# Where SyncE stores the x product in a graph kernel's loop: behind two groups of row copies or behind all four

## The chip, the cores and the metric

The kernel runs on one core of one Trainium2 chip. The metric is the device time of one execution in microseconds (us), and lower is better.

## The reference

Two graph layers, each followed by a residual and a layer norm over 256 features, for 12,500 nodes and 200,000 edges that are sorted by destination. The loop that the change touches belongs to the first layer:

```python
ZU = jnp.einsum('nd,kdr->knr', Z, U)            # 4 heads of 16 columns
zs = ZU[:, src, :]
zd = ZU[:, dst, :]
logits = (zs * zd).sum(-1) / scale
seg_max = jax.vmap(lambda l: jax.ops.segment_max(l, dst, num_segments=N))(logits)
exp_l = jnp.exp(logits - seg_max[:, dst])
seg_sum = jax.vmap(lambda e: jax.ops.segment_sum(e, dst, num_segments=N))(exp_l)
alpha = exp_l / (seg_sum[:, dst] + 1e-16)
weighted = alpha[..., None] * zs
agg = jax.vmap(lambda w_: jax.ops.segment_sum(w_, dst, num_segments=N))(weighted)
...
DZ = Z_half @ Dmat.T
residual = Z_half - DZ @ Dmat
grad_step = Z_half + ETA * (residual @ Dmat)
return jax.nn.relu(grad_step - ETA * LAM)
```

What `grad_step` does to Z itself, without the neighbours' part, is one product of x with a 256x256 matrix. It doesn't depend on the edges, and the kernel works it off inside the edge loop, two tiles of 128 nodes at a time. That is "the x product".

## The kernel before

The edges are cut into 1,563 tiles of 128. With the changes from one tile of nodes to the next the work has 1,660 steps, in 52 blocks of 32 steps, and a block has four groups of 8 steps (g = 0 to 3). One period of the loop on TensorE, VectorE and ScalarE is one block b:

- TensorE turns the block's logits around (L1384), which marks the start of a period here. VectorE runs a chain of short scans over them, with small steps of TensorE between (L1387 to L1398), until the exponents' arguments are ready (L1012, semaphore `x_ready`). Between the steps of the chain TensorE transposes the next block's one-hots (L1335).
- TensorE multiplies two tiles of x (L1378), and ScalarE copies the product out of PSUM (L1617, `xmz_copied`). VectorE scans the sums of the block before (L931), weighs the source rows and splits them in three bf16 parts (L1026, L1031, L1036).
- TensorE expands the next block's destination rows (L1347, 24 matmuls for each of four groups) and adds this block's rows up (L1364, eight quarters). The order written out is: expand 0 and 1, add up quarters 0 to 3, expand 2, quarters 4 and 5, expand 3, quarters 6 and 7. Two quarters belong to a group of 8 steps, and `sums_ps` counts quarters. Then the next period begins.

The source rows come in two moves. GpSimd gathers them from `z_table` in HBM with indirect DMAs, one for each edge tile (L576), in groups of 8, into a ring of 32 slots. SyncE (SP) copies them from the ring to the place in `zs` of each step (L437, 8 DMAs for a group). It can do so only when TensorE has added up what stood there two blocks before, so `copy_steps` waits for `sums_ps`, and when the gathered tiles have landed. After it has issued the copies of a group it waits until those of the group before have landed, and counts `copied` (L418). GpSimd waits for that count before it starts the next 8 gathers into the slots that came free (L573). So a group's gathers start when SP is done with a certain group of copies.

SP runs down one list. A `turn` is its share of a block. The turn of block b also loads the resets of block b (L453), stores the x product of period b - 1, for which it waits until ScalarE has copied it in that period (L470, L471), and loads the x tiles for the next product (L460).

Of the kernel before, what the change touches and what calls it, by code (L numbers as in the profile page):

```python
# [60 lines left out]
NG = B // G  # L61
# [36 lines left out]
def spread(ap, axis, n):  # L98

    shape = list(ap.shape)  # L100
    shape[axis] = n
    return ap.broadcast_to(shape)
# [25 lines left out]
def program(nc, x, xT, src_rows, dst_rows, u, dmat, head_w, weight, attn_l, attn_r, out):  # L128
    ctx = ExitStack()
    with ctx:  # L130
# [239 lines left out]
        def rows_of(table, t, n):  # L370

            return table[bass.ds(t * P, n * P), :].rearrange("(t p) c -> p t c", p=P)
# [17 lines left out]
        def _(sp):  # L390
# [24 lines left out]
            def landed(h, g, uses):  # L415

                sp.wait_ge(gathered[h][g], 16 * G * uses)
                sp.nop(nofuse=True).then_inc(copied, 1)  # L418

            def copy_steps(b, h, g, uses):  # L420

                start = type(b) is int and b < 2
                if not start:
                    sp.wait_ge(sums_ps, (B // Q) * (b - 2) + (B // Q // NG) * (g + 1))
                _, slots = nc.values_load_multi_w_load_instructions(
                    irow[0:1, bass.ds(b * B + g * G, G)], engines=[mybir.EngineType.SP], min_val=0, max_val=RING - 1,
                    skip_runtime_bounds_check_because="the vector engine has made them numbers of slots")
                if start and b == 0 and g == 0:
                    sp.wait_ge(tiles_in[0], 16 * G)
                else:  # L430
                    need = [sp.value_load(needs[0:1, bass.ds((b * NG + g) * 2 + i, 1)], min_val=16 * G, max_val=16 * G * EG) for i in range(2)]
                    for i in range(2):
                        sp.wait_ge(tiles_in[i], need[i])
                    sp.nop(nofuse=True)
                here = G if not (type(b) is int and b == NB - 1) else min(G, REAL - b * B - g * G)
                for j in range(here):
                    sp.dma_start(zs[:, h, g * G + j, 0:KR], ring[:, bass.ds(slots[j], 1), :].rearrange("p a c -> p (a c)")  # L437
                                 ).then_inc(gathered[h][g], 16)
                if g >= 1:
                    landed(h, g - 1, uses)  # L440
                elif not (start and b == 0):
                    landed(1 - h, NG - 1, uses - 1 if h == 0 else uses)
# [9 lines left out]
            def load_resets(b, h):  # L452
                sp.dma_start(resets[:, h, 0:P], spread(reset_rows[bass.ds(b * B, B), :].rearrange("j (a e) -> j a e", a=1), 1, K)  # L453
                             ).then_inc(resets_in[h], 16)
# [4 lines left out]
            def load_tiles(n, h):  # L459
                sp.dma_start(xe[:, h, :, :], xT[:, :, bass.ds(n * YT * P, YT * P)].rearrange("c p n -> p c n")).then_inc(xe_in[h], 16)  # L460

            def turn(b, h, uses, store, load):

                for g in range(2):
                    copy_steps(b, h, g, uses)
                sp.wait_ge(x_ready, b - 1)
                load_resets(b, h)
                if store:

                    sp.wait_ge(xmz_copied, b - 1)  # L470
                    sp.dma_start(rows_of(xmz_table, (b - 2) * YT, YT), xmz.rearrange("p (t d) -> p t d", t=YT)).then_inc(xmz_out, 16)  # L471
                if load:
                    load_tiles(b - 1, 1 - h)
                for g in range(2, NG):
                    copy_steps(b, h, g, uses)

            for g in range(2, NG):
                copy_steps(0, 0, g, 1)
# [4 lines left out]
            with nc.sync.Fori(1, NB // 2 - 2) as i:  # L483
                for h in range(2):
                    turn(2 * i + h, h, i + 1, True, True)
            for b in range(NB - 4, NB):
                turn(b, b % 2, b // 2 + 1, b - 2 < NY, b - 1 < NY)
# [1274 lines left out]
```

## Time and profile before

| | |
|---|---|
| median of 3 runs | 3708.65 us (3697.53 to 3719.24) |
| the profiled execution | 3677.74 us, of which span 3675.2 us |
| PE busy in the span | 1971.2 us (54%) |
| DVE busy | 1919.5 us (52%) |
| ACT busy | 1168.6 us (32%) |
| POOL busy | 1728.5 us (47%) |
| periods of the edge loop | 52 starts of a period, 193.3 to 3206.2 us |

No engine is busy for much over half of the span. Idle time of an engine says nothing by itself: what counts is which wait ends last in a period. The times of a timeline are microseconds from the start of the span, and the engine called SPq is SP's queue of DMA issues.

### The profile page before, as it was taken

The numbers are of one execution on the slowest core, as the hardware profiler recorded it, in microseconds if no ns is written. First come the engines' busy times: TensorE is split into PE (matmuls) and PEld (weight loads), VectorE is DVE, ScalarE is ACT, GpSimd is POOL, SyncE is SP. The second block draws the span as 40 slices with busy tenths as digits, with TensorE's granted clock in tenths as the row PEclk, the third lists the DMA queues.
The fourth block names the chain that finished last, engine by engine and source line by source line (L and its number), as shares of the span: only waits on it lengthen the run. The fifth ranks groups of instructions, "written<-read, shape, count | busy, mean of one in ns | idle before, by whom it ended". The sixth has DMA issues, their size and how long they took to land. (4 is left out here: it accounts for less than half of the span.)

```text
span 3675.2 us, 61713 instructions
## 1 busy us (share of the span) xinstructions
PE 1971.2 (54%) x15251; PEld 1490.8 (41%) x15252; DVE 1919.5 (52%) x5864; ACT 1168.6 (32%) x3040; POOL 1728.5 (47%) x1832
## 2 busy tenths in 40 slices
PE   9345545454545445454545455464545454567776
PEld 9233333343434334343424243343433333444666
DVE  4444646454545546454545455464545454666477
ACT  1112323222232323322232233233232322334477
POOL 1544454445444444554544544445544444252662
PEclk7555555555555555555555555555555555577798
DMA  6212222121212212121212112121212121285343
GB/s 205 52 32 46 47 44 46 42 46 42 48 41 47 46 41 48 42 49 40 47 39 48 42 44 48 41 50 41 48 40 45 41 49 39 58 274 179 112 140 107
DMA packets 406593, 232.96 MB, mean 63 GB/s; under 512 B 284096, under 2 KB 371434, under 8 KB 406506
## 3 DMA queue, kind: packets, MB, share of 16 engines
q1 hardware_dynamic: 346666, 154.11, 15.4%
q0 software_dynamic: 59840, 77.87, 9.8%
q8 instruction: 33, 0.54, 0.1%
q14 instruction: 54, 0.44, 0.0%
HBM read 134.80 MB, written 42.55 MB: 48 GB/s over the span
## 5 line engine op out<-in xcount | busy, mean ns | idle before, releaser
L576 POOL DMA_INDIRECT arena<-z_table,sslot x1563 | 1492.0, 955 | 1646.2 <-SPq L418 1114.0
L1347 PE MATMUL bank<-arena 128*128 x4992 | 613.8, 222 | 637.7 <-issue 585.8
L1347 PEld LDWEIGHTS bank<-arena 128*128 128x128 bf16 x4992 | 457.5, 105 | 789.5 <-issue 697.0
L1584 ACT ACTIVATE arena<-bank 128x272 f32<-128x272 f32 x416 | 269.8, 661 | 1574.8 <-remote 970.4
L902 DVE TENSOR_TENSOR xin<-arena,bank 128x512 f32<-128x512 f32 x208 | 143.1, 688 | 1044.3 <-remote 588.2
L1561 ACT ACTIVATE acc<-xTb 128x68 f32 x1600 | 384.6, 312 | 306.6 <-issue 296.0
L1364 PE MATMUL bank<-xto,arena 128*128 128x68 bf16 x3328 | 321.6, 246 | 147.5 <-issue 147.4
L1335 PE MATMUL bank<-ident_b,arena 128*128 128x128 bf16 x1664 | 214.8, 310 | 339.4 <-remote 205.3
L1364 PE MATMUL bank<-arena 128*128 128x68 bf16 x1664 | 296.9, 243 | 120.2 <-issue 90.5
L1364 PEld LDWEIGHTS bank<-xto,arena 128*128 128x128 bf16 x3328 | 281.5, 132 | 166.9 <-issue 166.9
L1335 PEld LDWEIGHTS bank<-ident_b,arena 128*128 128x128 bf16 x1664 | 160.4, 141 | 399.6 <-remote 200.2
L893 DVE TENSOR_SCALAR arena<-iota_b,didx 128x128 bf16<-128x128 bf16 x1664 | 297.9, 263 | 20.2 <-issue 13.4
L931 DVE TENSOR_TENSOR_SCAN xTb<-bank,arena 128x198 f32<-128x198 f32 x612 | 273.2, 522 | 16.2 <-ACT acc L1561 10.3
L1364 PEld LDWEIGHTS bank<-arena 128*128 128x128 bf16 x1664 | 214.1, 129 | 156.8 <-issue 117.9
L1571 ACT ACTIVATE arena<-bank 128x1024 bf16<-128x1024 bf16 x208 | 209.4, 1007 | 83.5 <-remote 52.0
L1378 PE MATMUL bank<-mz,dspace 128*128 128x256 f32 x392 | 183.4, 617 | 0.0
L1031 DVE TENSOR_TENSOR xto<-arena 128x544 f32<-128x544 f32 x208 | 149.3, 718 | 0.0
L905 DVE TENSOR_REDUCE agn<-xin 128x32 f32<-128x512 f32 x208 | 142.7, 686 | 7.2
L1036 DVE TENSOR_TENSOR xto<-xto 128x544 bf16<-128x544 f32 x208 | 145.3, 719 | 0.0
L1026 DVE TENSOR_TENSOR arena<-arena,bank 128x512 f32<-128x512 f32 x208 | 137.5, 681 | 1.8
L632 POOL DMA_INDIRECT xin<-xmz_table,src x98 | 95.4, 973 | 84.8 <-SPq L529 28.2
L1378 PEld LDWEIGHTS bank<-mz,dspace 128*128 128x128 f32 x392 | 109.4, 307 | 16.4
(264 smaller groups left out, 2543.6 us busy)
## 6 DMA issues: line engine op xcount, KB each, us to landing
arena<-arena SPq DMA_DIRECT2D x1660, 32.0 KB
arena<-z_table,sslot POOLq DMA_INDIRECT x1563
dspace<-in_xT SPq DMA_DIRECT2D x49, 256.0 KB
xmz_table<-agn SPq DMA_DIRECT2D x49, 256.0 KB
xmz_table<-arena SPq DMA_DIRECT2D x14, 896.0 KB
arena<-in_x SPq DMA_DIRECT2D x13, 896.0 KB, 11.4
out<-arena SPq DMA_DIRECT2D x12, 896.0 KB
xin<-in_xT SPq DMA_DIRECT2D x8, 896.0 KB
```

The lines of the kernel that those rows point to most:

```text
L576: pool.indirect_dma_start(ring[:, e % RING, :], None, z_table, bass.IndirectOffsetOnAxis(ap=sslot[:, e:e + 1], axis=0)).then_inc(tiles_in[ ...
L893: last = V.tensor_scalar(onehot[:, h, j, :], iota_b[:, :], didx[:, h, j:j + 1], None, ALU.is_equal)
L931: part_done = V.tensor_tensor_scan(to[:, c0:c1, :].rearrange("p c j -> p (c j)"), same_row[:, 0:(c1 - c0) * (B + 1)], sums[:, c0:c1, :].re ...
L1031: V.tensor_tensor(rest[:, js, :], zs[:, h, js, :], top(zs[:, h, js, :]), ALU.subtract).then_inc(rest_ready, 1)
L1036: V.tensor_tensor(low[:, js, :], rest[:, js, :], top(rest[:, js, :]), ALU.subtract).then_inc(parts_ready, 1)
L1335: last = T.transpose(tr_ps[g % 2][:, u * P:(u + 1) * P], onehot[:, h, g * G + u, :], ident_b[:, :])
L1347: last = T.matmul(zd_ps[g % 2][:, u * KR:(u + 1) * KR], onehotT[:, g * G + u, :], z3[:, bass.ds(tiles[u], 1), s, :].rearrange("p a c -> p ...
L1364: last = T.matmul(sum_ps[q % 2][:, (u % Q) * AW:(u % Q + 1) * AW], onehot[:, h, u, :], parts[s][:, u % Q, :], start=(s == 0), stop=(s == Z ...
L1378: last = T.matmul(zd_ps[1][:, t * D:(t + 1) * D], xe[:, 1 - h, c, t * P:(t + 1) * P], mz[:, c, :], start=(c == 0), stop=(c == DC - 1))
L1561: A.activation(acc[:, bass.ds(tiles[u % G], 1), :].rearrange("p a c -> p (a c)"), state[:, :, 1 + u], ACT.Copy).then_inc(state_stored, 1)
L1571: A.activation(onehotT[:, g * G:(g + 1) * G, :].rearrange("p j e -> p (j e)"), tr_ps[g % 2][:, :], ACT.Copy).then_inc(oneT_ready, 1)
L1584: A.activation(sums[:, :, 1 + q * Q:1 + (q + 1) * Q].rearrange("p c j -> p j c"), sum_ps[q % 2][:, 0:Q * AW].rearrange("p (j c) -> p j c", ...
```

## The change

In each turn SP issues the copies of all four groups first, and only then waits for the x product, stores it and loads the next x tiles. Nothing is added or left out, and no other engine's list changes.

```diff
                 sp.wait_ge(x_ready, b - 1)
                 load_resets(b, h)
+                for g in range(2, NG):
+                    copy_steps(b, h, g, uses)
                 if store:

                     sp.wait_ge(xmz_copied, b - 1)
                     sp.dma_start(rows_of(xmz_table, (b - 2) * YT, YT), xmz.rearrange("p (t d) -> p t d", t=YT)).then_inc(xmz_out, 16)
                 if load:
                     load_tiles(b - 1, 1 - h)
-                for g in range(2, NG):
-                    copy_steps(b, h, g, uses)
```

## Rows read from the trace of the kernel before

**Rows 1.** The page: the costliest group, busy us, mean ns, idle before.

```profile
L576 POOL DMA_INDIRECT arena<-z_table,sslot x1563 | 1492.0, 955 | 1646.2 <-SPq L418 1114.0
```

**Rows 2.** Waits of SP's queue, 200 to 3200 us: total us, times, longest.

```profile
SPq L471 <- ACT agn L1617: 309.0, 35, 26.9
...
SPq L434 <- DMA arena<-z_table,sslot: 4.4, 6, 1.1
```

**Rows 3.** Busy time by windows: the whole edge loop, and five of its periods.

```profile
193.30:3206.20 3012.90, 1518.39 (x12632) 1124.34 (x12632) 1534.25 (x4729) 879.19 (x2432) 1435.04 (x1507) 0.54 0.20 44
...
1613.00:1672.50 59.50, 30.45 (x249) 22.50 (x249) 30.28 (x94) 17.79 (x50) 30.33 (x32) 0.50 0.21 45
...
1916.00:1961.10 45.10, 28.88 (x248) 21.85 (x248) 30.41 (x94) 19.53 (x58) 17.25 (x18) 0.54 0.21 48
2156.40:2204.20 47.80, 29.11 (x249) 22.04 (x248) 29.92 (x94) 17.58 (x51) 23.27 (x24) 0.54 0.22 48
3036.70:3104.30 67.60, 29.87 (x249) 22.06 (x248) 30.17 (x94) 18.08 (x51) 30.46 (x32) 0.53 0.18 40
3171.10:3206.20 35.10, 26.98 (x240) 21.03 (x240) 29.91 (x94) 16.58 (x50) 2.50 (x3) 0.50 0.11 25
```

The columns are: window, its length, and the busy us with the instructions of PE, PEld, DVE, ACT and POOL, then the granted clock of PE, the DMA share and GB/s.

**Rows 4.** Busy time by windows inside the period from 1613.0 us.

```profile
1620.50:1628.00 7.50, 2.10 (x16) 1.83 (x17) 2.84 (x19) 1.92 (x5) 4.95 (x6) 0.50 0.27 55
...
1633.00:1641.00 8.00, 5.74 (x55) 4.45 (x54) 7.90 (x17) 0.60 (x1) 6.17 (x7) 0.50 0.35 90
...
1652.50:1669.00 16.50, 1.77 (x9) 0.89 (x9) 0.00 (x0) 0.65 (x1) 11.35 (x12) 0.50 0.19 36
```

**Rows 5.** Timeline of SP's DMA issues in that period, and one of 3069 us.

```profile
1611.33 5.07 SPq L437 DMA_DIRECT2D arena<-arena  x8
1619.93 8.91 SPq L437 DMA_DIRECT2D arena<-arena  x8
1629.04 0.63 SPq L453 DMA_DIRECT2D xTb<-reset_rows  x1
1634.78 0.41 SPq L471 DMA_DIRECT2D xmz_table<-agn  x1
1641.45 5.47 SPq L437 DMA_DIRECT2D arena<-arena  x8
1649.73 7.62 SPq L437 DMA_DIRECT2D arena<-arena  x8
1670.92 5.08 SPq L437 DMA_DIRECT2D arena<-arena  x8
...
3069.06 0.39 SPq L471 DMA_DIRECT2D xmz_table<-agn  x1
```

**Rows 6.** Timeline of GpSimd in that period: first and last gathers.

```profile
1617.23 0.95 POOL L576 DMA_INDIRECT arena<-z_table,sslot  x1 [9.25 <-SPq L418]
...
1629.59 0.95 POOL L576 DMA_INDIRECT arena<-z_table,sslot  x1 [2.61 <-SPq L418]
...
1647.76 0.94 POOL L576 DMA_INDIRECT arena<-z_table,sslot  x1 [6.51 <-SPq L418]
...
1666.52 0.94 POOL L576 DMA_INDIRECT arena<-z_table,sslot  x1 [0.30 <-issue]
```

**Rows 7.** Timeline of VectorE in that period.

```profile
1629.71 0.29 DVE L1012 TENSOR_TENSOR xin<-bank,xin 128x128 f32<-128x128 f32 x1
...
1644.12 0.22 DVE L1054 TENSOR_SCALAR fac<-bank,first_col 128x4 f32<-128x4 f32 x1
```

**Rows 8.** Timeline of TensorE in that period.

```profile
1612.98 0.47 PE L1384 MATMUL bank<-ident,agn 128*128 128x128 f32 x1
...
1646.11 3.16 PE L1347 MATMUL bank<-arena 128*128 x24
...
1661.58 0.21 PE L1347 MATMUL bank<-arena 128*128 x1 [1.88 <-issue]
```

**Rows 9.** Busy time by windows of the gathers (L576) alone.

```profile
3036.70:3056.70 20.00, 15.06 (x16) 0.50 0.21 43
```

## The prediction

> **What bounds the kernel now.** The page comes first. No engine is busy for more than 54% of the span, so the loop is held by waits, and the costliest group on the page is GpSimd's gathers: 955 ns each, and most of their idle time ends with SP's count of landed copies [rows 1]. The windows come next. The edge loop takes 3012.9 us, 51 periods of 59.1 us, with 29.5 gathers in each [rows 3]. The five single periods have nearly the same work on PE, DVE and ACT and very different lengths. With 3 gathers (and no x product) a period takes 35.1 us, with 18 it takes 45.1, with 24 it takes 47.8, with 32 it takes 59.5, and with 32 at other places 67.6 [rows 3]. So a period is some 35 to 38 us of chained work plus what the gathers take away, and it matters where they fall.
>
> The windows inside one period show how they take it. From 1652.5 to 1669.0 us, under 12 gathers, PE gets 9 matmuls done in 16.5 us and DVE nothing [rows 4]. One matmul of the expansion stands alone, 1.88 us behind the one before, for which the profile has no reason but "issue", where 24 of them took 3.16 us a few us earlier [rows 8]. SP is slowed as well: eight copies take 5.07 us in the open and 8.91 or 7.62 us under gathers, and from the end of one group at 1657.35 to the next at 1670.92 it needs 13.6 us, where it took 3.5 us from 1616.40 to 1619.93 [rows 5]. The start of the slow time lags the first gather: gathers start at 1647.76 and PE goes on until about 1651. Its end lags the last one: 1666.52, and PE moves again at about 1669 [rows 4, 6]. So I take each run of 8 gathers as 10 us, of which the first 3.5 are free and 2.5 behind it are not, some 8 to 9 us of slow time. A run that directly follows another gets no free start.
>
> What a slow time costs depends on what it meets. Count from the period's start at 1613.0 [rows 8]. Up to `x_ready` at 17 (1629.99) a chain of short steps runs, and there it costs its full length: in the window from 7.5 to 15 PE got 16 matmuls and DVE 19 instructions done [rows 4]. From 17 to 31 DVE works through long instructions (1629.71 to 1644.12, [rows 7]) and PE has only two expansions and some adding to do. Under the gathers from 16.6 on, DVE is busy for 7.90 of 8.0 us and PE does 55 matmuls [rows 4]: this run is nearly free. Then PE has four quarters, two expansions and four quarters to do, some 12 us in the open, and the 16 gathers from 34.8 to 54.5 stop it. Of four runs of 8 one is free, one costs 8 us in the chain, and two cost some 16 us in front of the period's end. 36 and 24 make 60, as measured.
>
> **The change part by part.** No instruction is added or removed. In each turn one wait, one store and one load (0.41 us for the issue of the store, and the load is alike) move behind two groups of copies, 16 copy issues and two headers.
>
> The wait itself: SP stood in it for 309.0 us, 35 times, 8.8 us each [rows 2]. In this period SP is done with the resets at 1629.67 and stores at 1634.78, so 5.1 us [rows 5]. After the change groups 2 and 3 don't wait for it. What they then wait for is `sums_ps` of two blocks before, long reached, and gathered tiles. Those waits are 4.4 us in the whole loop now [rows 2]; a group needs the gathers that started three or four groups of copies earlier, so I take 0 to 1 us a period and keep 2 as the upper bound. The group that is moved up starts at about 1632.5 in place of 1641.45.
>
> Who is waiting for SP's copies? GpSimd, and nobody else near: DVE and PE read a block's last copies at the end of the period, 15 us after SP has issued them (1657.35, next period at 1672.5), and after the change they come sooner still. So 5.1 us saved on SP save nothing directly. They move gathers. The store and the load are late by some 20 us at most; the next product is wanted a period later, so that is 0, and if the cover went it would be at most the delay of one x product, 5 us a period.
>
> Where the gathers go. From one group 0 to the next SP takes 59.6 us (1611.33 to 1670.92, [rows 5]), so without the wait some 54.5, so SP runs ahead until another wait holds it. That is the wait of group 0 for the sums of the first two quarters that PE makes in the present period. The expansion behind the first four quarters starts at 33.1 [rows 8], so these sums are there at about 32, 15 us behind `x_ready`. From that moment (called 0) I walk through one turn with the durations above. SP: header 2.2, copies 5.1, first gathers at 8.3. PE, undisturbed, ends its period some 12 us after those sums (the period of 45.1 us, whose gathers were out of its way, less 33), just as the slow time sets in at 12. Group 1 is issued by 20, with gathers at 21; group 2 by 32, gathers at 33; group 3 by 45, gathers at 45.5. So slow times lie at 12 to 20, 25 to 32, 36.5 to 44.5 and 49 to 57. The chain to `x_ready` needs 17 - 7.5 = 9.5 us in the open. It starts at 12 and gets 0, 5 and 4.5 us in the gaps, 9.5 together. It ends either at about 36.5 or, if that gap is missed, at 45. In the first case the slow time from 36.5 is free, but the one from 49 meets PE's expansions, and the sums come at about 60. In the second DVE's 14.5 us run from 45 to 59.5, the last slow time is mostly free, and PE's remaining 3 to 5 us behind 57 put the sums at 60 to 64. The new period is thus 60 to 64 us in place of 59.5, or up to 69 where PE misses its end before 12 and loses the first slow time as well. I take 61.5, 2 us more: the two runs of gathers that met PE's last part now meet the chain, which is no cheaper, and the free run stays about as free. Periods with 24 gathers should move by as much. 49 turns store an x product: 49 x 2 = 98 us.
>
> The bounds. Upper: the period from 3036.7 has 16 gathers in its first 20 us [rows 9] and stores x at 32.4 in place of 21.8 [rows 5]; with 67.6 us [rows 3] it is 8 us longer than the common one. If half of the turns look like that, 24 x 8 = 192 us more, and if all do, 390. Lower: two free runs in place of one, 8 us less in a third of the turns, 130 us less. The sum is made for the profiled execution: 3677.7 + 98 = 3776. The median of the runs lies 31 us above it, so 3807; I round to 3800.
>
> By the Trainium skill (SBUF — State Buffer, "SBUF: two separate sides") a DMA can't be slowed by a compute instruction nor the other way round, and only GpSimd and VectorE lock each other out of a shared pair of ports. What stands in [rows 4] disagrees: TensorE, which by that page waits for nobody, issues 9 matmuls in 16.5 us. By the page the place of the gathers wouldn't matter and the change would be worth nothing, which is the second rival's time.
>
> **The rivals.** *Faster: SP's wait was holding the gathers back, and they land better.* GpSimd idles for 6.5 us before its gathers at 1647.76 [rows 6] because SP has waited for x and then copied group 2, and most of that is in the time in which DVE has its long instructions. If groups 2 and 3 are gathered in that stretch, two of four runs are free. It decides if SP does not run ahead to the sums but stays about 10 us earlier than now. A second free run is worth up to 8 us in 32; with a third to a half of the turns that is 130 to 190 us: about 3550. Against it: gathers from 28 on then join those before them without a free start, and SP's cycle of 54.5 us won't stay in step with a period of under 60.
>
> *No change: the gathers cost the same wherever they fall.* The period with 24 gathers and that with 32 cost 1.99 and 1.86 us for each gather. If only the number counts, and it stays, the time does: 3709. Against it stand two periods with 32 gathers each and 8 us between them [rows 3].
>
> *Much slower: all four runs meet the chain and PE's end.* It takes that PE misses its end by a microsecond when SP's group 0 is released by PE itself: 67 to 69 us a period, 8 x 49 = 390 us, about 4100. For it: the two events fall together in my walk. Against it: PE also feels 3.5 us of free start, and such a lock would repeat only in turns with all 32 gathers.
>
> **How the numbers follow.** Forecast (0.5 to 5% slower) 0.42, much slower 0.12, no change 0.13, faster 0.33. 0.5%, or 19 us, is about what a measurement of this kernel can tell. The forecast's own range is 3730 to 3900. For 8 in 10 I leave out most of the much slower case and the far end of the faster one: 3590 to 3970. Faster 0.33, same 0.13, slower 0.54.
>
> **What would show it.** In the profile after: SP's wait at L471 shrinks, and a wait of group 0 for `sums_ps` (L425, on PE L1364) takes its place; that row right means that SP ran ahead. The gathers of a period start in four separate runs and none of 16. The store of x lies 30 us or more behind a period's start instead of 22. PE's stretch behind the first four quarters is free of gathers. If SP still waits at L471 and never at L425, SP did not run ahead and the walk is wrong. If the runs of gathers lie in the 15 us behind `x_ready`, the faster rival holds. If waits at L434 reach some us a period, the ring of 32 slots sets the pace and my 0 to 1 us was wrong.

## The result and the profile after

The changed kernel takes 3798.88 us in the median of 3 runs (3791.43 to 3809.05), against 3708.65 before: a ratio of 1.0246 (95% interval 1.0185 to 1.0308). It is slower, by 90 us. The forecast was 3800, in a range of 3590 to 3970.

The profiled execution took 3791.43 us, span 3789.5. The edge loop, in the windows view with the columns of [rows 3], and then five stretches of its common period, which starts at 1602.9 us:

```profile
178.10:3317.30 3139.20, 1492.44 (x12632) 1126.50 (x12632) 1530.42 (x4729) 875.69 (x2432) 1437.23 (x1507) 0.53 0.19 42
...
1602.90:1666.20 63.30, 29.11 (x250) 22.33 (x249) 30.05 (x94) 17.36 (x49) 30.58 (x33) 0.53 0.19 43
1604.00:1621.50 17.50, 0.00 (x0) 0.00 (x0) 0.00 (x0) 0.87 (x2) 12.17 (x13) 0.50 0.20 41
1621.50:1629.40 7.90, 3.55 (x21) 2.36 (x22) 5.55 (x28) 5.49 (x21) 0.00 (x0) 0.50 0.15 32
1629.40:1641.00 11.60, 8.35 (x38) 5.62 (x36) 6.33 (x33) 5.69 (x19) 7.55 (x8) 0.50 0.19 38
1643.30:1655.00 11.70, 4.67 (x48) 3.75 (x48) 10.92 (x22) 0.14 (x1) 7.55 (x8) 0.61 0.26 67
1655.00:1666.20 11.20, 10.61 (x121) 9.11 (x121) 4.82 (x8) 3.64 (x6) 2.48 (x3) 0.50 0.13 29
```

The loop is 126.3 us longer (3139.2 against 3012.9, [rows 3]), with the same instructions and nearly the same busy times (PE 1492 us against 1518, the others within 4). It also began 15 us earlier (178.1 against 193.3), which nothing in the change touches. The span grew by 114.3. The common period went from 59.5 to 63.3 us. In its first stretch TensorE and VectorE don't issue one instruction in 17.5 us, while GpSimd issues 13 gathers. In the last one PE goes at full rate: 121 matmuls in 11.2 us, where [rows 4] had 9 in 16.5.

SP's waits from 200 to 3320 us (total us, times, longest):

```profile
SPq L425 <- PE bank L1364: 262.5, 37, 10.8
SPq L425 <- remote: 139.0, 13, 12.6
SPq L473 <- ACT agn L1617: 91.0, 23, 17.8
...
SPq L434 <- DMA arena<-z_table,sslot: 2.6, 4, 1.4
```

The wait for the x product (309.0 us in [rows 2], now at L473) fell to 91.0. In its place SP waits 401.5 us at L425, which is the wait for the sums of the present period. All of it is in front of group 0. Gathered tiles are waited for no more than before (2.6 us against 4.4).

The timelines of SP, of the starts of GpSimd's runs of gathers, of VectorE's `x_ready` and last step (L1012, L1054), and of PE's period starts:

```profile
1602.21 4.54 SPq L437 DMA_DIRECT2D arena<-arena  x8
...
1623.50 5.11 SPq L437 DMA_DIRECT2D arena<-arena  x8
1632.20 10.23 SPq L437 DMA_DIRECT2D arena<-arena  x8
...
1643.14 0.42 SPq L473 DMA_DIRECT2D xmz_table<-agn  x1
...
1657.18 5.11 SPq L437 DMA_DIRECT2D arena<-arena  x8
```

```profile
1600.16 0.94 POOL L576 DMA_INDIRECT arena<-z_table,sslot  x1 [11.77 <-SPq L418]
...
1629.43 0.94 POOL L576 DMA_INDIRECT arena<-z_table,sslot  x1 [9.60 <-SPq L418]
...
1643.26 0.94 POOL L576 DMA_INDIRECT arena<-z_table,sslot  x1 [4.15 <-SPq L418]
...
1663.11 0.94 POOL L576 DMA_INDIRECT arena<-z_table,sslot  x1 [10.12 <-SPq L418]
```

```profile
1637.49 0.29 DVE L1012 TENSOR_TENSOR xin<-bank,xin 128x128 f32<-128x128 f32 x1
...
1653.36 0.21 DVE L1054 TENSOR_SCALAR fac<-bank,first_col 128x4 f32<-128x4 f32 x1
```

```profile
1602.89 0.48 PE L1384 MATMUL bank<-ident,agn 128*128 128x128 f32 x1
...
1666.19 0.47 PE L1384 MATMUL bank<-ident,agn 128*128 128x128 f32 x1
```

Group 0 of the next turn is now copied at 1657.18, 9 us ahead of the period's end at 1666.19. Its release starts 8 gathers 3 us ahead of that end (1663.11, and 1600.16 for the period shown). Group 1 follows at full pace at 1602.21, and the 8 gathers it releases join the first 8: one run of 16 gathers until 1619.8, across the start of the chain. With `x_ready` taken at the start of L1012, it comes 34.6 us behind the period's start, against 16.7 before ([rows 7, 8]). The run from 1643.26 falls under VectorE's long instructions, and from `x_ready` to the end it takes 28.7 us, against 42.8.

The common period is no exception. With a period's start taken at L1384 and its `x_ready` at L1012, in 47 periods of each trace (the fourth to the fiftieth):

| | start to `x_ready`, mean | rest, mean | periods with over 22 us to `x_ready` |
|---|---|---|---|
| before | 18.3 us | 41.1 us | 7 |
| after | 31.7 us | 30.6 us | 40 |

The first part lost 13.4 us a period and the second won 10.5. The long ones, of over 22 us, are those that a long run of gathers meets. In the changed kernel's trace a run of more than 8 gathers (with under 1 us between two of them) reaches into the part up to `x_ready` in 40 periods, and these are the same 40. Before, it does so in 10 periods, and all 7 long ones are among them.

### The profile page after: what moved, and what is told of

Read it like the earlier page. It is cut to its first block, busy times and chain, and to the rows that moved or that the text cites. A ratio compares the mean times of both kernels' runs of the same rounds, so it can differ in the third digit from the quotient of the medians.

```text
span 3789.5 us, 61713 instructions
## 1 busy us (share of the span) xinstructions
PE 1924.7 (51%) x15251; PEld 1474.1 (39%) x15252; DVE 1915.1 (51%) x5864; ACT 1164.2 (31%) x3040; POOL 1729.0 (46%) x1832
## 4 chain that ended last, share of the span: by engine, by line
another core or an unknown queue 17%; PE 16%; DVE 10%; issue 7%; ACT 3%; ACTq 1%; DMA 0%; POOL 0%; DVEq 0%; POOLq 0%; SPq 0%
PE bank L1347 5%; PE bank L1364 3%; DVE arena L893 2%; PE bank L1502 2%; DVE xTb L931 2%; PE bank L1472 1%; PE bank L1492 1%; PE bank L1504 1%; PE bank L1378 1%; ACT arena L1661 1%; PE bank L1476 1%; ACT acc L1561 1%; DVE xto L1031 1%; PE bank L1335 1%
## 5 line engine op out<-in xcount | busy, mean ns | idle before, releaser
L576 POOL DMA_INDIRECT arena<-z_table,sslot x1563 | 1494.4, 956 | 1749.0 <-SPq L418 1227.9
L1347 PE MATMUL bank<-arena 128*128 x4992 | 598.5, 226 | 247.8 <-issue 201.9
L1347 PEld LDWEIGHTS bank<-arena 128*128 128x128 bf16 x4992 | 464.8, 107 | 390.4 <-issue 292.6
L1387 PE MATMUL bank<-ident,xin 128*1 128x128 f32 x104 | 30.5, 395 | 747.1 <-DVE xin L970 692.9
L970 DVE TENSOR_TENSOR_SCAN xin<-xTb,bank 128x128 f32<-128x128 f32 x52 | 21.9, 420 | 740.0 <-remote 728.1
L1364 PE MATMUL bank<-xto,arena 128*128 128x68 bf16 x3328 | 312.7, 246 | 31.0 <-issue 30.9
L1364 PEld LDWEIGHTS bank<-arena 128*128 128x128 bf16 x1664 | 215.1, 129 | 183.6 <-issue 91.4
```

The source lines that it names most:

```text
L576: pool.indirect_dma_start(ring[:, e % RING, :], None, z_table, bass.IndirectOffsetOnAxis(ap=sslot[:, e:e + 1], axis=0)).then_inc(tiles_in[ ...
L1347: last = T.matmul(zd_ps[g % 2][:, u * KR:(u + 1) * KR], onehotT[:, g * G + u, :], z3[:, bass.ds(tiles[u], 1), s, :].rearrange("p a c -> p ...
L1364: last = T.matmul(sum_ps[q % 2][:, (u % Q) * AW:(u % Q + 1) * AW], onehot[:, h, u, :], parts[s][:, u % Q, :], start=(s == 0), stop=(s == Z ...
```

## The experiments

Ratios are to the kernel before on the same chip, with a 95% interval. The medians of before there were 3660 to 3674 us. The changed kernel itself wasn't run again beside them.

**Groups 2 and 3 held back again, store and load left late.**

```diff
-                sp.wait_ge(x_ready, b - 1)
+                if store:
+                    sp.wait_ge(xmz_copied, b - 1)
+                else:
+                    sp.wait_ge(x_ready, b - 1)
                 load_resets(b, h)
                 for g in range(2, NG):
                     copy_steps(b, h, g, uses)
```

> The changed kernel, with the resets' load between groups 1 and 2 waiting for the x product of the present period (xmz_copied) instead of for x_ready of the one before. So groups 2 and 3 are held as in the kernel before, but store and load of x stay behind group 3. If the change costs time because SP runs ahead and its gathers land in the chain, the ratio to before is 0.995 to 1.005 and L425 holds SP for under 50 us. If the late store and load cost the time, the ratio stays at 1.02 or more.

Measured 3655.97 us, ratio 0.9949 (0.9897 to 1.0001). The waits of SP's queue:

```profile
SPq L453 <- ACT agn L1620: 288.6, 30, 27.3
SPq L434 <- DMA arena<-z_table,sslot: 14.2, 18, 1.4
SPq L425 <- remote: 13.6, 2, 12.2
SPq L425 <- PE bank L1367: 1.5, 5, 0.6
```

The wait for the product is back (288.6 us), the wait for sums is nearly gone (15.1 us), and so is the loss. In the common period the store now goes out about 47 us behind the start, later than in the changed kernel (40 us), and it costs nothing. So the late store and load are not the cause.

**Groups 2 and 3 held only until the present `x_ready`.**

```diff
-                sp.wait_ge(x_ready, b - 1)
+                sp.wait_ge(x_ready, b)
                 load_resets(b, h)
```

> The changed kernel, with the resets' load between groups 1 and 2 waiting for x_ready of the present period, which is some 5 us ahead of the product's copy. Groups 2 and 3 so come some 8 us sooner than before and can't come sooner than that. If it counts where the gathers land, more of them lie in VectorE's long instructions: ratio 0.97 to 0.995. If only running ahead to the sums costs, 1.00. If each us by which the groups come sooner costs, 1.005 to 1.02.

Measured 3755.07 us, ratio 1.0182 (1.0097 to 1.0267). Here my expectation of a gain fell. The ratio lies in the range that I had given for a cost of each us by which the groups come sooner, but the periods show another course. Groups 2 and 3 are copied at 25 and 33 us in place of 29 and 37, and with them group 0 comes at 54 to 55 in place of 58. That is enough for its gathers to begin before the period's end in part of the periods: 17 of 47 have over 22 us to `x_ready`, against 7 before and 40 after. Most of the other periods with 32 gathers take about 60 us, no less than before. The starts of gather runs in one of the bad periods, from 1827.8 us:

```profile
1824.74 0.95 POOL L576 DMA_INDIRECT arena<-z_table,sslot  x1 [11.19 <-SPq L418]
...
1867.46 1.32 POOL L576 DMA_INDIRECT arena<-z_table,sslot  x1 [23.00 <-SPq L418]
```

One run of 16 gathers over the start, again, and the period took 69.6 us.

**Store and load between the third and the fourth group.**

```diff
                 load_resets(b, h)
+                copy_steps(b, h, 2, uses)
                 if store:
...
                     load_tiles(b - 1, 1 - h)
-                for g in range(2, NG):
-                    copy_steps(b, h, g, uses)
+                copy_steps(b, h, 3, uses)
```

> Half of the change: store and load stand between group 2 and group 3. Group 2 isn't held by x, group 3 is. If SP's running ahead is what costs, SP still stops at x each period, the runs of gathers differ little from before, and the time is 3690 to 3740 us. If the time goes up with each group that is put ahead of the store, about 3750.

Measured 3667.6 us, ratio 1.0002 (0.9965 to 1.0039). SP still stops at x (252.9 us, 29 times), and 7 of 47 periods have a long chain, as before. Its copies stand at the places of before, but each place has the group that comes one further down the list: groups 1 and 2 around the period's start (at -1.8 and 7.6 us in the median), then the store, then group 3 at 29.4 and group 0 of the next turn at 37.2, some 22 us ahead of the period's end. So a group 0 that goes out early costs nothing by itself, and the cost doesn't grow group by group: half of the change is free. SP's list in its common period, from 1534.7 to 1595.2 us:

```profile
1532.98 5.07 SPq L437 DMA_DIRECT2D arena<-arena  x8
1538.49 0.63 SPq L453 DMA_DIRECT2D xTb<-reset_rows  x1
1542.47 9.69 SPq L437 DMA_DIRECT2D arena<-arena  x8
...
1556.75 0.41 SPq L472 DMA_DIRECT2D xmz_table<-agn  x1
...
1564.47 5.12 SPq L437 DMA_DIRECT2D arena<-arena  x8
1572.45 6.93 SPq L437 DMA_DIRECT2D arena<-arena  x8
```

The load of the resets (L453) marks the first of these groups as group 1, and the store (L472) the second as group 2.

**The other direction: store and load between the first and the second group.**

> The other direction: store and load of x between group 0 and group 1, so three groups of copies stand behind the wait for x. SP can run ahead less than before. If every place that keeps a wait for x within reach of SP is alike, the ratio is 0.995 to 1.01. If the place sets where the runs of gathers fall and the kernel before had a good one, it is 1.01 to 1.06.

The load of the resets stays behind group 1. Measured 3933.83 us, ratio 1.0775 (1.0693 to 1.0856), beyond the 1.06 that I had as the upper end, and by another mechanism than the one I had named. Who waited for SP's copies (total us, times):

```profile
  DVE xin L902: 817.0, 86
```

Before it was 23.4 us in 5 times. SP waits 776.2 us for x and has three groups to copy behind it, so VectorE waits for the copies themselves. The part behind `x_ready` is 4.3 us longer than before (45.4 us in the mean), and the part up to it 1.3.

**Group 0 held until the period's end.** The changed kernel, with this wait in `copy_steps`, and as its control the kernel before with the same:

```diff
-                    sp.wait_ge(sums_ps, (B // Q) * (b - 2) + (B // Q // NG) * (g + 1))
+                    sp.wait_ge(sums_ps, (B // Q) * (b - 2) + (B // Q if g == 0 else (B // Q // NG) * (g + 1)))
```

> The changed kernel, with group 0 of a turn waiting for all eight quarters of the sums of the present period instead of two. Groups 1, 2 and 3 are as early as the order allows. If the change costs because group 0 is copied some 5 us ahead of the period's end, so that 16 gathers run without a gap over the start of the chain, this takes the cost away though groups 2 and 3 still go ahead of the x product: ratio to before 0.98 to 1.005. If it costs because groups 2 and 3 go ahead of the x product, the ratio stays at 1.015 or more, and if the longer wait costs by itself, it is over 1.025.

> The kernel before with the same wait of group 0, as a control. Its group 0 is mostly copied at the period's end anyway (57 to 60 us behind the start), so I expect 0.99 to 1.005. If the longer wait costs by itself, it is 1.01 or more.

Measured: the changed order with the hold 3703.44 us, ratio 1.0088 (1.0051 to 1.0124); the order of before with the hold 3710.46, ratio 1.0103 (1.0066 to 1.0140). The hold costs about 1% by itself, more than I expected of it. The 1.0088 alone lies in none of the ranges that I had named; it is the control that decides. With the hold the two orders are alike, and the changed one loses nothing. What the hold takes away is not group 0's lead alone: SP issues the groups in order, so groups 0 to 3 of the changed order all come later than without it, at 2.1, 10.8, 24.1 and 40.8 us in place of -8.7, -0.7, 20.5 and 28.7. The starts of gather runs in its common period, which starts at 1514.6 us:

```profile
1522.79 0.94 POOL L576 DMA_INDIRECT arena<-z_table,sslot  x1 [16.99 <-SPq L418]
1535.93 0.94 POOL L576 DMA_INDIRECT arena<-z_table,sslot  x1 [3.35 <-SPq L418]
1563.82 0.94 POOL L576 DMA_INDIRECT arena<-z_table,sslot  x1 [7.81 <-SPq L418]
```

The first gathers come 8 us behind the start and no longer 3 us ahead of it. `x_ready` comes 11.5 us behind the start in the mean, and no period has over 22. The 16 gathers in one run from 1535.93 then fall into the second part. Against the kernel before, the first part is 6.8 us shorter and the second 8.0 longer (49.1 us in the mean), which is what the hold loses.

**The hold with the store between the third and the fourth group.**

> Store between groups 2 and 3 with the same wait of group 0. If the ends of periods are kept free of gathers by this and one group more comes in VectorE's long instructions, 0.97 to 0.995; if it does the same as without the wait, 1.00.

Measured 3657.68 us, ratio 0.9948 (0.9913 to 0.9983). It is half a per cent faster than the kernel before, at the upper end of what was expected. Why the hold costs 1% in the two kernels above and nothing here, I can't show.

**Half of the gathers left out.** In both kernels GpSimd fetches only every second edge tile (with a memset of the ring to zero at the start, and all thresholds cut accordingly):

```diff
-                for e in range(q * G, min((q + 1) * G, ET)):
+                for e in range(q * G, min((q + 1) * G, ET), 2):
```

> The kernel before with every second gather left out (edge tiles 1, 3, 5 of each group of 8 and so on are never fetched, their ring slots keep zeros; all copies, waits and other work stay). If gathers take time from the other engines, a period falls from 59 to about 45 us and the time to 2950 to 3100 us. If the rows' slow times have another cause than gathers, it stays above 3500.

> The changed kernel with the same half of the gathers left out. If the change costs because of where the gathers land, the distance to the kernel before with half the gathers shrinks from some 90 to at most 45 us. If the order on SP and its waits for the sums cost by themselves, the distance stays 90 us or more.

Measured: 2673.4 us for the order of before, ratio 0.7289 (0.7261 to 0.7318), and 2619.18 us for the changed one, ratio 0.7142 (0.7043 to 0.7240). The edge loops of the two:

```profile
138.80:2192.10 2053.30, 1477.65 (x12633) 1130.99 (x12633) 1525.21 (x4729) 860.21 (x2432) 717.13 (x754) 0.53 0.23 52
```

```profile
138.90:2137.80 1998.90, 1474.30 (x12633) 1126.78 (x12633) 1525.66 (x4729) 852.07 (x2432) 728.61 (x754) 0.54 0.23 53
```

All other engines do the same work in 2053 us in place of 3013. For 781 gathers left out the time fell by 993 us (3666.87 - 2673.4), 1.27 us for each, about the distance at which GpSimd issues them in a run (16 in 20.0 us, [rows 9]). And the change has turned its sign: with half of the gathers it makes the kernel 54 us faster, though SP waits for the sums there too (L426, 216.2 us). I had only expected the loss to shrink. The wait for sums, then, isn't what costs. Nor is the early place of the copies: they go out at -9.1 and -1.1 us there, as in the changed kernel, and `x_ready` comes at 13.3 us in the mean, with no period over 22.

## Why the prediction was right

**SP runs ahead until the sums of the present period hold it: right.** The row that I had named is there, 401.5 us at L425, all of it in front of group 0. The store went out about 40 us behind a period's start, and TensorE's stretch behind the first four quarters is nearly free of gathers, as I had written. Tiles were not the limit (2.6 us), and the late store and load cost nothing, as the run with the product's hold shows.

**Gathers stop the other engines: right, and shown.** Half of the gathers gone took 27% of the time, with the same work on all other engines. TensorE and VectorE had no instruction at all in 17.5 us under gathers. The Trainium skill's rule that a DMA can't be slowed by a compute instruction or the other way round (SBUF — State Buffer, "SBUF: two separate sides") would have made the place of the gathers indifferent. The traces disagree: in the 47 periods the part up to `x_ready` is 31.7 us in the changed kernel, where the long runs of gathers lie in it, against 18.3 before.

**The free run: right in this period.** From 1643.3 to 1655.0 VectorE is busy for 10.92 of 11.7 us with 8 gathers beside it. The faster rival built on more of it, and the run held at `x_ready` was a test of it: its groups 2 and 3 came 4 us sooner, and the undisturbed periods gained nothing. What is left of that rival is the half per cent of the hold with the store after the third group.

**The walk through one turn: right in its outcome, wrong in one place.** It had four separate runs of gathers, with 3.5 us of free start each, and wrote that none of 16 would be seen. Group 1 in fact is copied at full pace right at the period's start, so its gathers join those of group 0. The chain gets no gap in them: `x_ready` at 34.6 us where the walk, with period start at 12, had 24.5 or 33. The common period is 63.3 us, in the 60 to 64 of the walk, but I had taken 61.5.

**The slow time was read too early.** I had taken 3.5 us from the first gather to its start, with TensorE going on until about 1651. That trace has TensorE at full rate until 1652.57, 4.8 us behind the first gather at 1647.76, and again from 1670.69, not 1669. In the common period after the change it was 3 us.

```profile
1650.59 1.98 PE L1347 MATMUL bank<-arena 128*128 x15
1652.92 0.21 PE L1347 MATMUL bank<-arena 128*128 x1 [0.36 <-issue]
...
1670.69 0.23 PE L1364 MATMUL bank<-arena 128*128 128x68 bf16 x1 [1.19 <-issue]
```

**The term that was mis-sized** is this one: 2 us for each of 49 turns, 98 us. The loop grew by 126.3 us, 2.6 a turn. The span grew by only 114.3, mostly because the part ahead of the loop was 15 us shorter in that execution. From one profiled execution to the other the time grew by 113.7 us (3677.74 to 3791.43), 16 more than my 98. In return I had added 31 us for the distance from the profiled execution to the median, and after the change that distance was 7. The two misses nearly cancel, so that the forecast of 3800 came within 2 us of the measured 3798.88 is luck.

**What the cause is.** The table has the times at which SP's four groups of copies go out, from the start of a period (a minus is ahead of it; medians), and the two parts of a period (means), all in us and over the same 47 periods:

| | copies around the start | copies later | to `x_ready` | rest |
|---|---|---|---|---|
| before | -1.6, 6.5 | 29.6, 37.4 | 18.3 | 41.1 |
| changed | -8.7, -0.7 | 20.5, 28.7 | 31.7 | 30.6 |
| changed, product's hold | -1.1, 7.0 | 29.5, 37.2 | 17.2 | 41.8 |
| changed, hold at `x_ready` | -6.6, 1.4 | 25.4, 33.2 | 20.3 | 41.2 |
| store after the third group | -1.8, 7.6 | 29.4, 37.2 | 17.9 | 41.2 |
| store after the first group | 0.0 | 30.7, 39.4, 56.6 | 19.6 | 45.4 |
| changed, group 0 held | 2.1, 10.8 | 24.1, 40.8 | 11.5 | 49.1 |
| before, group 0 held | 2.2, 10.9 | 26.3, 37.3 | 11.7 | 48.7 |
| store after the third group, group 0 held | 2.2, 10.9 | 24.1, 43.3 | 12.7 | 46.8 |
| before, half of the gathers | -0.5, 7.7 | 24.2, 32.1 | 14.1 | 26.4 |
| changed, half of the gathers | -9.1, -1.1 | 8.2, 16.4 | 13.3 | 26.1 |

The loss of the changed kernel appears where the two groups around the period's start go out 5 to 7 us sooner than before, whichever groups these are, so that the gathers behind them join over the start of the chain. It appears in the changed kernel and, less, with the hold at `x_ready`. It is absent with the product's hold and with the store after the third group, where the copies stand at the places of before. It is absent where group 0 is held, against its control. And it is absent with half of the gathers, though the copies come as early as in the changed kernel. The store's place costs nothing by itself: SP's stop at the product is the brake that keeps it from running ahead. Why the hold costs 1% in two orders and nothing with the store after the third group is open.

## What to carry to other kernels

A wait on a queue that is done with its work early can be the pacing of something that disturbs everybody: before moving it, ask what the queue will trigger sooner and on whose critical stretch that falls. Where one kind of transfer stops all engines, count the periods by where its runs fall, not by their number alone. And give a hold its control: the same hold in the unchanged kernel cost as much as the change with it seemed to.

## What the hardware showed unexpectedly

Under the gathers of 128 rows of 256 bytes all engines' instructions come slowly, SP's too (one each 0.7 to 1.4 us from 1607.8 to 1623.5 in the period shown), though DMA traffic is small (a share of 0.19 to 0.20 in the period's slow windows). A group of 8 copies took 10.23 us there and 4.54 to 5.11 where it went at full pace. TensorE and VectorE stopped some 3 us behind the first gather of the common period after (1600.16), while SP issued its 8 copies at full pace until 1606.75. VectorE moved again at 1623.61, 3.8 us behind the end of the last gather. In the period of [rows 4] TensorE slowed 4.8 us behind the first gather and was back 3.2 us behind the end of the last. What is shared between them, whether the way of the descriptors, of the instructions, the profiler's own recording or something else, no run here tells; a gather of narrower rows wasn't tried.
